# Local attention on one core: maximum as Exp bias, split float32r projections, scores moved ahead of the output projection

## What is computed

```python
h = shift_token(x)                      # second half of the features from the token before
q, k, v = split(h @ wqkv)               # 128 -> 3 x 512, 8 heads of 64
q = l2norm(q) * qs; k = l2norm(k) * ksc
q, k = rotary_xpos(q, k)
sim = einsum('bhwid,bhwjd->bhwij', q * 8, [k of the window before, k])   # windows of 64, keys 128
sim = where((i < j) | (i > j + 64) | (j == -1), -max, sim)
o = softmax(sim) @ [v of the window before, v]
x = x + o @ wo
h = layernorm(shift_token(x)) @ w1 + b1
x = x + (a * gelu(g)) @ w2 + b2         # a, g the halves of h
```

## Time and profile before

| | |
|---|---|
| median of 3 runs | 1563.13 us |
| profiled execution | 1563.58 us, its span 1561.7 us, granted clock 0.947 |
| busy, share of the span | PE 1346.8 us (86%), DVE 1145.6 (73%), ACT 801.7 (51%), POOL 724.0 (46%) |
| stretch 900 to 1000 us (attention, layer 0) | PE 95.69, DVE 87.56, ACT 70.77, POOL 63.40, clock 1.00 |
| stretch 1200 to 1300 us (attention, layer 1) | PE 95.82, DVE 87.52, ACT 70.80, POOL 64.26, clock 1.00 |
| local transformer | about 705 to 1561.7 us; its units 0 to 31 about 739 to 1057 and 1155 to 1473 |

### The profile page before, as it was taken

One profiled execution on the slowest core, in us unless ns is written; L12 is line 12 of the kernel. 1 busy time (PEld: TensorE's weight loads), 2 busy tenths in 40 slices (PEclk: granted clock), 3 DMA queues, 4 the chain that ended last, 5 costly groups with the idle time before them and its releaser, 6 DMA issues.

```text
span 1561.7 us, 39029 instructions
## 1 busy us (share of the span) xinstructions
PE 1346.8 (86%) x15968; PEld 970.4 (62%) x15968; DVE 1145.6 (73%) x2484; ACT 801.7 (51%) x1633; POOL 724.0 (46%) x562
## 2 busy tenths in 40 slices
PE   4545999988999999984999999967989999998797
PEld 3434878875777777762666666654556666665554
DVE  3776776434888888874888888864578888888565
ACT  1222223224666666653777777742457777776421
POOL 1752545541344433434666666632246666666100
PEclk7776999996999999997999999999999999999999
DMA  4000544500000000003000100011100000000011
GB/s 133 0 0 16 112 93 110 108 13 2 3 3 3 4 3 3 3 3 91 8 8 7 22 8 8 1 30 28 25 24 8 9 17 13 9 5 2 12 31 54
DMA packets 61837, 40.34 MB, mean 26 GB/s; under 512 B 41312, under 2 KB 51808, under 8 KB 61664
## 3 DMA queue, kind: packets, MB, share of 16 engines
q1 hardware_dynamic: 61664, 37.88, 10.2%
HBM read 27.12 MB, written 2.36 MB: 19 GB/s over the span
## 4 chain that ended last, share of the span: by engine, by line
PE 33%; ACT 8%; SPq 6%; DVE 4%; POOL 2%; issue 1%; DMA 1%; DVEq 0%; POOLq 0%; ACTq 0%
PE PS L1872 7%; SPq L1463 5%; PE PS L1923 5%; PE PS L1957 4%; PE PS L1914 4%; PE PS L1891 3%; PE PS L1937 2%; ACT e_oT L1787 2%; PE PS L1948 2%; ACT qk L1756 2%; ACT e_pm L1793 2%; PE PS L1907 2%; POOL rot L1537 2%; PE PS L2010 1%; PE PS L2019 1%
## 5 line engine op out<-in xcount | busy, mean ns | idle before, releaser
L1537 POOL TENSOR_TENSOR rot<-qk,sinl 128x1024 f32<-128x1024 f32 x64 | 217.6, 3401 | 139.4 <-DVE qk L1631 139.4
L1530 POOL TENSOR_TENSOR rn<-ss,neghalf 128x16 f32<-128x16 f32 x64 | 185.6, 2901 | 108.6 <-DVE ss L1624 108.6
L1756 ACT ACTIVATE qk<-PS 128x512 f32<-128x512 f32 x128 | 76.4, 597 | 135.7 <-PE PS L1872 135.7
L1102 DVE TENSOR_REDUCE d_mx<-PS 128x4 f32<-128x576 f32 x128 | 96.9, 757 | 66.3 <-PE PS L1246 63.3
L1872 PE MATMUL PS<-wqkv,hT 128*128 128x512 f32 x256 | 128.8, 626 | 10.9 <-DMA qks<-in_e_ks 5.7
L607 POOL TENSOR_TENSOR uu<-uu,cb 128x512 f32<-128x512 f32 x64 | 82.8, 1295 | 90.0 <-DVE uu L839 88.2
L1923 PE MATMUL PS<-ident,e_pm 128*128 128x128 f32 x512 | 84.5, 289 | 45.9 <-ACT e_pm L1793 44.3
L1923 PEld LDWEIGHTS PS<-ident,e_pm 128*128 128x128 f32 x512 | 55.9, 144 | 102.4 <-ACT e_pm L1793 95.7
L739 ACT ACTIVATE sg<-PS 128x512 f32<-128x512 f32 x72 | 43.0, 597 | 134.1 <-PE PS L667 133.0
L1165 ACT ACTIVATE pa<-PS 128x512 f32<-128x512 f32 x128 | 76.5, 597 | 61.8 <-PE PS L1255 61.7
L1610 DVE TENSOR_REDUCE e_mx<-PS 128x8 f32<-128x1024 f32 x64 | 78.2, 1222 | 30.7 <-PE PS L1914 30.6
(11 more groups left out here) (241 smaller groups left out, 3535.9 us busy)
## 6 DMA issues: line engine op xcount, KB each, us to landing
cb<-comb_rows SPq DMA_DIRECT2D x32, 512.0 KB, 9.1
X<-in_L_attn_x SPq DMA_DIRECT2D x4, 512.0 KB, 7.4
zs<-Z SPq DMA_DIRECT2D x64, 32.0 KB
zg<-Z SPq DMA_DIRECT2D x16, 128.0 KB
out_x<-X SPq DMA_DIRECT2D x8, 256.0 KB, 2.5
zs<-Z SPq DMA_DIRECT2D x64, 31.8 KB
zg<-Z SPq DMA_DIRECT2D x16, 127.0 KB
wqkv<-in_e_wqkv SPq DMA_DIRECT2D x2, 768.0 KB, 4.2
```

The source lines that it names most:

```text
L1102: chain(dve.tensor_reduce(mx[:, par, :, :], s, AX.X, ALU.max))
L1530: pool.tensor_tensor(rn[:, v % 2, :], ss[:, v % 2, :], c.neghalf[:, :], ALU.pow).then_inc(rn_ready.sem, 1)
L1537: pool.tensor_tensor(rot[:, :, :, :], x, bc(sinl[:, t, :, :], 2, H2), ALU.mult).then_inc(rot_ready.sem, 1)
L1756: last = act.activation(qk[:, v % 4, s, :, :].rearrange("p h e -> p (h e)"), PS[:, QBANK + s, :], ACT.Copy)
```

## The change

The hidden features and wqkv are each split into a high part, rounded by ACT on its copy, and a low part, the difference, taken by DVE (features, and the first layer's weights) or POOL (the second layer's weights, in the feed-forward groups 0 to 2). Each projection becomes three float32r matmuls. The maximum is written negated and used as the bias of the Exp, which reads the scores in PSUM; a bias is one value per partition, so there is one Exp per head. The scores of unit u+1 are computed in step u, between weigh(u,1) and project_o(u-1). ACT takes q's half, exponentiates the first half, then takes k's half; take_qk comes before take_o. The buffers mask32 and zero move into the space of hT.

```diff
+        w_hi, w_lo = ssb("wqkv_hi", [P, 3 * INNER], F32R), ssb("wqkv_lo", [P, 3 * INNER], F32R)
+        h_hi, h_lo = ssb("e_h_hi", [P, 4, P], F32R), ssb("e_h_lo", [P, 4, P], F32R)
...
-        mx = ssb("e_mx", [P, 2, 4])
+        mx = ssb("e_mx", [P, 2, 2, 4])
...
 # SP, load_projections
-                        sp.wait_ge(ev_psum.sem, ev_psum.at(nunits * L))
+                        sp.wait_ge(wlo_ready.sem, wlo_ready.at(3 * L))
...
 # POOL
+                def split_weights(L, k):
+                    pool.wait_ge(whi_ready.sem, whi_ready.at(3 * L + k + 1))
+                    pool.tensor_tensor(w_lo[:, third(k)], wqkv[:, third(k)], w_hi[:, third(k)], ALU.subtract).then_inc(wlo_ready.sem, 1)
...
                             tables(L + 1, g)
+                            split_weights(L + 1, g)
                         if g + 2 < G:
                             rstd(L, g + 2)
...
 # DVE
-                def shift(L, v):
+                def low(L, v):
+                    dve.wait_ge(eh_ready.sem, eh_ready.at(n(L, v)))
+                    dve.tensor_tensor(h_lo[:, v % 4, :], PS[:, QBANK, 0:P], h_hi[:, v % 4, :], ALU.subtract).then_inc(el_ready.sem, 1)
+
+                def maxima(L, v):
                     dve.wait_ge(s_ready.sem, s_ready.at(n(L, v)))
+                    if n(L, v) > 2:
+                        dve.wait_ge(p_exp.sem, p_exp.at(2 * (n(L, v) - 2)))
                     s = PS[:, SBANK:SBANK + 2, :].rearrange("p r (j k) -> p r j k", k=2 * W2)
-                    steps(dve.tensor_reduce(mx[:, :, :], s, AX.X, ALU.max))
-                    for h in range(2):
-                        if n(L, v) > 2:
-                            dve.wait_ge(pT_psum.sem, pT_psum.at(2 * (n(L, v) - 2) - 1 + h))
-                        dve.tensor_tensor(pm[:, v % 2, h, :, :, :], s[:, :, 2 * h:2 * h + 2, :],
-                                          bc(mx[:, :, 2 * h:2 * h + 2], 3, 2 * W2), ALU.subtract).then_inc(p_shifted.sem, 1)
+                    dve.tensor_reduce(mx[:, v % 2, :, :], s, AX.X, ALU.max, negate=True).then_inc(max_ready.sem, 1)
...
                 def attend(L, u):
+                    if has(u + 4) and (u >= 0 or L == 0):
+                        low(L, u + 4)
                     if has(u):
-                        shift(L, u)
+                        maxima(L, u)
...
                     for g in range(G):
+                        if L + 1 < DEPTH and lead(g) is not None:
+                            low(L + 1, lead(g) + 4)
                         gated(L, g, 0)
...
 # ACT
+                def round_weights(L, k):
...
+                    act.activation(w_hi[:, third(k)], wqkv[:, third(k)], ACT.Copy).then_inc(whi_ready.sem, 1)
...
                 def exponent(L, v, h):
-                    act.wait_ge(p_shifted.sem, p_shifted.at(2 * n(L, v) - 1 + h))
-                    p = pm[:, v % 2, h, :, :, :].rearrange("p r j k -> p (r j k)")
-                    act.activation(p, p, ACT.Exp).then_inc(p_exp.sem, 1)
+                    if h == 0:
+                        act.wait_ge(max_ready.sem, max_ready.at(n(L, v)))
+                    if n(L, v) > 2:
+                        act.wait_ge(pT_psum.sem, pT_psum.at(2 * (n(L, v) - 2) - 1 + h))
+                    for r in range(2):
+                        for j in range(2):
+                            at = 2 * h + j
+                            last = act.activation(pm[:, v % 2, h, r, j, :], PS[:, SBANK + r, at * KEYS2:(at + 1) * KEYS2], ACT.Exp,
+                                                  bias=mx[:, v % 2, r, at:at + 1])
+                    last.then_inc(p_exp.sem, 1)
...
                         if u >= 0 or L == 0:
                             features(L, u + 4)
-                        take_features(L, u + 4)
+                        take_features(L, u + 4, 0)
                     if has(u):
                         exponent(L, u, 0)
+                    if has(u + 4):
+                        take_features(L, u + 4, 1)
+                    if has(u):
                         exponent(L, u, 1)
                         take_p(L, u, 0)
...
                         take_p(L, u, 1)
+                    if has(u + 1):
+                        take_qk(L, u + 1)
                     if has(u - 1):
                         take_o(L, u - 1)
-                    if has(u + 1):
-                        take_qk(L, u + 1)
...
 # PE
+                def project(to, v, k):
+                    pe.matmul(to, h_hi[:, v % 4, :], w_hi[:, third(k)], start=True, stop=False)
+                    pe.matmul(to, h_hi[:, v % 4, :], w_lo[:, third(k)], start=False, stop=False)
+                    return pe.matmul(to, h_lo[:, v % 4, :], w_hi[:, third(k)], start=False, stop=True)
+
                 def project_qk(L, v):
-                    pe.wait_ge(eh_ready.sem, eh_ready.at(n(L, v)))
...
+                    pe.wait_ge(el_ready.sem, el_ready.at(n(L, v)))
...
                 def scores(L, v):
...
-                        pe.wait_ge(p_shifted.sem, p_shifted.at(2 * n(L, v - 1)))
+                        pe.wait_ge(p_exp.sem, p_exp.at(2 * n(L, v - 1)))
...
                 def attend(L, u):
-                    if has(u):
-                        scores(L, u)
+                    if L and u == 0:
+                        scores(L, 0)
                     if has(u + 4):
                         project_qk(L, u + 4)
...
                         weigh(L, u, 1)
+                    if has(u + 1) and (u >= 0 or L == 0):
+                        scores(L, u + 1)
                     if has(u - 1):
                         project_o(L, u - 1)
                     if has(u + 5):
                         turn_z(L, u + 5)
```

More of the change, by code:

```diff
@@ L1367, in local_transformer @@
         sinl = ssb("sinl", [P, TB, 2, DH2])
-        mask32 = ssb("e_mask32", [P, 2, KEYS2])
+        mask32 = c.hT[:, 1, 0:2 * KEYS2].rearrange("p (m k) -> p m k", k=KEYS2)
         mask = ssb("e_mask", [P, 2, KEYS2], BF16)
-        zero = ssb("zero", [P, B, half])
+        zero = c.hT[:, 0, 0:B * half].rearrange("p (b d) -> p b d", d=half)
         zs = ssb("zs", [P, B, D])
@@ L1710, in _ @@
                 dve.wait_ge(qkv_loaded.sem, qkv_loaded.at(16 * 3))
+                for k in range(3):
+                    dve.wait_ge(whi_ready.sem, whi_ready.at(k + 1))
+                    dve.tensor_tensor(w_lo[:, third(k)], wqkv[:, third(k)], w_hi[:, third(k)], ALU.subtract).then_inc(wlo_ready.sem, 1)
                 dve.wait_ge(consts.sem, 48)
@@ L1750, in features, with take_features @@
                     act.wait_ge(zsT_psum.sem, zsT_psum.at(n(L, v)))
-                    act.activation(h_of(v), PS[:, QBANK, 0:P], ACT.Copy).then_inc(eh_ready.sem, 1)
-                def take_features(L, v):
-                    for s in range(2):
-                        act.wait_ge(eqkv_ready.sem, eqkv_ready.at(2 * n(L, v) - 1 + s))
-                        last = act.activation(qk[:, v % 4, s, :, :].rearrange("p h e -> p (h e)"), PS[:, QBANK + s, :], ACT.Copy)
-                    last.then_inc(qk_taken.sem, 1)
+                    act.activation(h_hi[:, v % 4, :], PS[:, QBANK, 0:P], ACT.Copy).then_inc(eh_ready.sem, 1)
+                def round_weights(L, k):
+                    if k == 0:
+                        act.wait_ge(qkv_loaded.sem, qkv_loaded.at(16 * 3 * (L + 1)))
+                        if L:
+                            act.wait_ge(ev_psum.sem, ev_psum.at(nunits * L))
+                    act.activation(w_hi[:, third(k)], wqkv[:, third(k)], ACT.Copy).then_inc(whi_ready.sem, 1)
+                def take_features(L, v, s):
+                    act.wait_ge(eqkv_ready.sem, eqkv_ready.at(2 * n(L, v) - 1 + s))
+                    act.activation(qk[:, v % 4, s, :, :].rearrange("p h e -> p (h e)"), PS[:, QBANK + s, :],
+                                   ACT.Copy).then_inc(qk_taken.sem, 1)
                 def squares(L, v):
-                    act.wait_ge(qk_taken.sem, qk_taken.at(n(L, v)))
+                    act.wait_ge(qk_taken.sem, qk_taken.at(2 * n(L, v)))
                     if n(L, v) > 1:
@@ L1834, in gelu @@
                        .then_inc(gelu_ready.sem, 1)
+                for k in range(3):
+                    round_weights(0, k)
                 for L in range(DEPTH):
@@ L1849, in _ @@
                         gelu(L, g, 2)
+                        if L + 1 < DEPTH and g < 3:
+                            round_weights(L + 1, g)
                         if L + 1 < DEPTH and lead(g) is not None:
@@ L1865, in turn_z @@
                     pe.transpose(PS[:, QBANK, 0:P], zs[:, b, :], ident[:, :]).then_inc(zsT_psum.sem, 1)
+                def project(to, v, k):
+                    pe.matmul(to, h_hi[:, v % 4, :], w_hi[:, third(k)], start=True, stop=False)
+                    pe.matmul(to, h_hi[:, v % 4, :], w_lo[:, third(k)], start=False, stop=False)
+                    return pe.matmul(to, h_lo[:, v % 4, :], w_hi[:, third(k)], start=False, stop=True)
                 def project_qk(L, v):
```

(14 more changed lines are left out.)

15 lines of the change are left out of this document (8 added, 7 removed).

## The result

The changed kernel takes 1620.22 us (median of 4 runs, 1616.71 to 1626.48) against 1562.23 us (4 runs, 1560.78 to 1567.19) for the kernel before: ratio 1.037, interval 1.034 to 1.040. The forecast was 1626 us. The profiled execution of the kernel after took 1626.48 us, its span 1624.7.

What follows compares the result with a forecast made beforehand. PE's own issue, some 9.1 of 9.85 us per unit, was the bound, with a chain through ACT in one place. 59 + 3 + 1 = 63 us on 1563.58 gave 1626 us; range 1588 to 1662; 1600 to 1665 had chance 0.65.

Steps and rivals of the forecast that it cites:

- now 2.1 after: Second turn_p of a unit on PE: waits for take_p(0), starting 2.1 us after the first instead of 1.44.
- The size of a unit: Attention unit, turn_z to turn_z: pitch goes from 9.85 to 10.90 us, +1.05 us, 56 times.
- 0.28 per instruction in a row: ACT's small Exps with bias: 0.28 us each in a row, 0.37 for the last, 1.12 of queue per half.
- 0.16 us per projection: Projections on PE: three float32r matmuls take 0.69 us instead of 0.85, saving 0.5 us per unit.
- The start: Before the first projection: one rounding and one subtraction more, one pass less: +1 us, between 0 and 2.
- One rounding and one subtraction: Start of the attention: the first projection waits for one rounding (0.6 us) and one subtraction (0.6 us).
- the clock falls: Rival: PE, idle some 1.7 us in 10.9, falls to 1.2 GHz; up to +3.5 us per unit, 1800 us; chance 0.04.
- The ends of the layers: Last four units of each layer: maximum waits for the residual sum, second Exp is longer: +0.4 x 8 = +3 us.
- the 56 units: Attention units with a projection for unit u+4, 28 per layer: +1.05 us each, +59 us.
- The feed-forward part: Second layer's weight split, where PE waits for loads of zs: nothing or up to +3 us; taken as 0.
- the rival's end of 0.7: Cheaper Exp on ACT: 0.7 us per half, pitch 10.05, 1579 us; chance 0.15 for below 1600.
- PE stays the bound: Rival: no wait before project_qk, Exp ready when PE comes; -0.7 us per unit, 1524 us; chance 0.06.

Runs made afterwards that it cites:

- after_front: The changed kernel with DVE's first subtraction of features (unit 0) ahead of the mask and the cosine and sine tables: 1614.24 us (one run).
- f32r_only: The kernel before with the float32r split and projections alone; old orders, subtractions on DVE, one Exp per half: 1566.10 us, ratio 1.001.
- bias_only: The kernel before with the maximum as bias alone, eight Exps of 128x128 per unit: 1595.85 us, ratio 1.020.
- order_only: The kernel before with the order alone: scores(u+1) ahead of project_o(u-1), take_qk ahead of take_o: 1594.97 us, ratio 1.020.
- turnz_bias: Changed kernel with turn_z(u+5) ahead of scores(u+1) and project_o(u-1), DVE's subtraction at step's end, residual sum after maxima, first subtraction ahead of tables: 1558.34 us, ratio 0.996.
- best3: As turnz_wide_clamp, with the residual sum between the maximum and its subtractions on DVE: 1543.48 us, ratio 0.985.
- turnz_wide_clamp: As turnz_bias, with the maximum subtracted on DVE, one Exp per half, and clamp(u+3) ahead of rotated(u+2) on DVE: 1543.58 us, ratio 0.987.
- best4: As best3, with the clamp of the sums of squares moved from DVE to POOL ahead of its power: 1541.88 us, ratio 0.984.

## Why the prediction was right or wrong

**Right: direction, and where it comes from.** "These 1.56 us" of scores over the copy of the features were the cover, and without them PE stands 0.69 us (predicted 0.7) before the projection. Of the steps counted from turn_z, features came at 0.31 (predicted 0.35), the projection at 0.96 (1.04), the first evacuation at 1.97 (2.03), the first Exp at 2.46 (2.52). The second turn_p waits for take_p(0), and it starts 2.09 us after the first, as "now 2.1 after" had it. PE then runs without a wait from turn_p(1) to turn_z: 8.12 for scores (8.35), 9.69 for project_o (9.91).

**The size of a unit: +1.05 predicted, +0.84 measured.** The term that was mis-sized is the Exp, "0.28 per instruction in a row". In a row they start 0.25 apart, and the evacuation follows 1.00 us after the first Exp, not 1.12; over two halves that is 0.24. take_p(0) starts at 4.93 (predicted 5.25), itself takes 0.67 and not 0.60, and 0.21 of the lead is left at the next turn_z. PE's waits are shorter than forecast by the same: 0.35 and 0.45 us before the two turn_p, not 0.6 and 0.7. The length of one was predicted as 0.37 and is 0.394: its own length does not tell the distance of two starts. By the Trainium skill (ScalarE: Activation LUTs, What ACT_TABLE_LOAD costs) 280 ns and 0.833 ns per element make an estimate of 387 ns, which agrees with 394. By its overlap of 93 ns the starts would be 0.29 us apart, also an estimate, and here the trace does not agree: 0.25.

**Float32r: 0.16 us per projection held, its gain per unit did not.** Starts are 0.23 us apart (928.58, 928.81), as in the earlier trace rows, and the first half was complete when the sum said. But the PE time that it saves lies in front of a wait: alone it gave 0.23 us of 0.5, because turn_p waits for the Exp (0.33 of the 0.5 reach it) and because its subtraction queues on DVE (0.1 on average). The Trainium skill (FP8 and Floating Point Precision, TensorE Precision Notes) gives true FP32 four passes; that a float32r matmul is a single one it does not say in so many words, only that the 4-byte value is read and truncated. Three passes against four would make a projection 0.64 us, an estimate; three starts of 0.23 make 0.69, and the trace's row was the one to take.

**The start: +1 predicted, +8.9 measured.** "One rounding and one subtraction" (1.2 us) was the step that failed, in three ways. Three of each stand ahead of the first projection, 2.9 us even in after_front. The subtraction of the features is queued on DVE behind 2.6 us of mask and tables (717.6 to 720.2), and the predicted range of 0 to 2 had no queue in it. And the first units, with their float32r passes and their waits, ran at a granted clock of 0.67 where the kernel before had 0.84. f32r_only has 7.1 of the 8.9 us by itself, bias_only 0.9 and order_only none. The rival "the clock falls" was put into the steady units, where it did not happen (1.00 from 900 to 1000 us):

```profile
900.00:1000.00 100.00, 86.19 (x983) 63.82 (x981) 70.80 (x122) 73.31 (x181) 58.57 (x19) 1.00 0.06 17
```

**The ends of the layers: +3 predicted, +9 measured in the profiled execution** (+11 by the table, but two of the 56 units lie in them, 1.7 us). The queue was foreseen correctly: in the first unit of the tail the maximum starts 2.97 us after scores (1042.28, 1045.25) and in the kernel before 1.70 (1015.02, 1016.72), predicted 3.0 and 1.7. In the next, shown below, DVE takes 1.2 us of statistics first in both kernels: 4.17 (1051.69, 1055.86) and 2.81 (1024.34, 1027.15). And 1.0 us of project_o is not paid later. What was left out is the clock. First the kernel before, a unit in the tail:

```profile
1024.34 0.59 PE L1907 MATMUL PS<-e_mask,identb 128*128 128x512 bf16 x2
...
1029.78 0.66 PE L1923 MATMUL PS<-ident,e_pm 128*128 128x128 f32 x4 [3.82 <-ACT e_pm L1793]
```

then the kernel after:

```profile
1051.69 0.61 PE L1948 MATMUL PS<-e_mask,identb 128*128 128x512 bf16 x2
...
1058.27 1.11 PE L1964 MATMUL PS<-ident,e_pm 128*128 128x128 f32 x4 [3.85 <-ACT e_pm L1820]
1059.18 1.91 PE L1932 MATMUL PS<-ident,qk 128*128 128x128 f32 x8
```

After a wait of 3.8 us the transposes take 1.11 instead of 0.66 us: 1.2 GHz. The kernel before falls to it too, but less long: the granted clock of this unit and the next is 0.73 and 0.74 after, 0.86 and 0.85 before, and they take 12.6 and 13.1 us, not 11.9 and 11.2. How much of the 9 us is the clock, after_front shows, whose code is the same here. There the unit after the one shown, and the stretch from it to the first Gelu, read (busy times, then the granted clock):

```profile
1062.80:1074.70 11.90, 8.04 (x99) 6.75 (x96) 3.89 (x15) 4.50 (x13) 1.21 (x2) 0.86 0.03 5
1074.70:1089.50 14.80, 10.83 (x117) 7.93 (x116) 3.60 (x10) 6.75 (x16) 0.00 (x0) 1.00 0.00 1
```

In the kernel after the same unit takes 13.1 us at 0.74, and the stretch behind it

```profile
1077.30:1094.80 17.50, 13.61 (x120) 10.28 (x116) 3.62 (x10) 6.42 (x15) 0.00 (x0) 0.80 0.00 1
```

With both layers the ends of after_front are 4.0 us longer than those of the kernel before, 2.3 without the two units: close to the predicted 3. So +9 is the price of the change in an execution with a low clock there, and +2 in one where it was higher. What it is on average two profiles cannot tell.

**The feed-forward part: 0 predicted, -0.4 and +1.6 measured,** which is within what these stretches differ between kernels.

The errors have opposite signs. The 56 units were 14 us too dear (59 against 43.3 + 1.7), the start 8 us too cheap, and in the profiled execution the other stretches another 6 together. So the 63 us of that execution are met exactly, and the median, 1620.22 us, is missed by 6. That the total came out nearer than its terms is luck; direction and mechanism of the unit are not.

**Rivals.** The Exp was cheaper than forecast by 0.12 us per half (1.00 against 1.12), far from the rival's end of 0.7. "PE stays the bound" needed 0.7 us of PE work between turn_z and the projection. The new order has none; turnz_bias put it there, with two DVE steps and the first subtraction moved too, and the loss of 3.7% turned into a gain of 0.4%.

## What to carry to other kernels

Before a step moves, write down which latency it covers where it stands: here 1.56 us of scores hid the copy, and would have hidden the subtraction. Moving them cost about as much as the bias (taken back they give 32 and 29 us), while moving turn_z in front of them gained. Shortening an engine that no one waits for (DVE's two subtractions) at the price of more instructions on an engine in the chain (six more Exps) is a loss. And price the ramp at the start and the tails by the queues and the clock that they have, not by the steady unit.

## What the runs showed of the hardware that was not expected

**DVE waits for POOL in some operations.** The clamp, 128x16 with two operands in SBUF, takes 0.17 us after by_sine. Issued beside it, in best3 and turnz_wide_clamp, it takes 0.66 and 0.55 us and ends at 911.87 and 909.62, 0.03 and 0.04 us after by_sine (911.84, 909.58). best3, DVE and POOL:

```profile
911.21 0.66 DVE L1638 TENSOR_TENSOR ss<-ss,tiny 128x16 f32<-128x16 f32 x1
...
908.43 3.41 POOL L1540 TENSOR_TENSOR rot<-qk,sinl 128x1024 f32<-128x1024 f32 x1 [2.48 <-DVE qk L1645]
911.95 3.38 POOL L1533 TENSOR_TENSOR rn<-ss,neghalf 128x16 f32<-128x16 f32 x1
```

POOL is held too: its power takes 2.90 us alone and 3.38, 3.38 and 3.21 in turnz_wide_clamp, best3 and best4, where it starts beside DVE's sums, and in all three it ends 2.13 to 2.16 us after the second sum. The Trainium skill (SBUF — State Buffer, SBUF: two separate sides) says that a DVE operation with two inputs in SBUF and a GpSimd operation that reads SBUF exclude each other for their whole length; the rows of the clamp agree, which ends with by_sine. The power is held by 0.31 to 0.48 us only, less than the 1.3 us of the two sums beside it, which no row explains. No run was made for this alone, and what by_sine's own 3.40 us hold of such a wait (it starts beside DVE's product with the cosine) no row tells.

**Float32r at 1.2 GHz.** At the lower clock a pass of 512 columns costs 0.43 us, so a projection at the start of the stage costs about 1.3 us instead of 0.69, and starting the units 3.1 us earlier gained 1.1 us.
